# Two tiles of ternary weights move to the upper end of SBUF

## What is computed

```python
x = layernorm(x + attention0(x))      # causal softmax, 16 heads
x = layernorm(x + ffn0(x))            # ternary weights, below
x = layernorm(x + attention1(x))      # linear attention, relu features
x = layernorm(x + ffn1(x))            # plain weights

def ternarize(W):
    mask = abs(W) > 0.05 * max(abs(W))
    alpha = sum(abs(W) * mask) / max(sum(mask), 1)
    return alpha * sign(W) * mask     # alpha, 0 or -alpha

def ffn0(x):                          # W1 is 2048 x 512, W2 is 512 x 2048
    h = gelu(x @ ternarize(W1).T + b1)
    y = h @ ternarize(W2).T + b2
    scale = max(abs(y)) / 7 + 1e-8
    return clip(round(y / scale), -7, 7) * scale
```

## The kernel before

| phase | weights | activations | left over 512: weights, activations |
|---|---|---|---|
| qkv0 | p1_w_hi 33,472; p1_w_lo 58,048 | p1_xT_hi 90,816; p1_xT_lo 107,200 | 192, 192 |
| out0 | p3_w_hi 107,232; p3_w_lo 115,424 | p3_o_hi 140,000; p3_o_lo 156,384 | 224, 224 |
| ffn0 | tern 17,088 | p4_xT_hi 101,152; p4_xT_lo 117,536; p4_h_hi 138,016; p4_h_lo 142,112 | 192, 288 |
| linear attention | p5_w_hi 25,248; p5_w_lo 58,016 | p5_aT_hi 131,744; p5_aT_lo 148,128 | 160, 160 |
| ffn1 | p6_w0_hi 25,248; p6_w1_hi 90,784 | p6_xT 184,992; p6_h 203,424 | 160, 160 |

## Time and profile before

### The profile page before, as it was taken

One profiled execution on the slowest core, in us unless ns is written; L12 is line 12 of the kernel. 1 busy time (PEld: TensorE's weight loads), 2 busy tenths in 40 slices (PEclk: granted clock), 3 DMA queues, 4 the chain that ended last, 5 costly groups with the idle time before them and its releaser, 6 DMA issues. The chain is left out here.

```text
span 2647.1 us, 39886 instructions
## 1 busy us (share of the span) xinstructions
PE 2425.0 (92%) x12832; PEld 1797.7 (68%) x12832; DVE 1218.3 (46%) x2491; ACT 819.4 (31%) x1371; POOL 911.5 (34%) x1099
## 2 busy tenths in 40 slices
PE   7999699999999968599999994799999979999997
PEld 5888455555555436478888883588888858888886
DVE  3333477777777759611111112767677362111121
ACT  3222055555555531043344432111101112222221
POOL 0000156556556545233333332525153222222221
PEclk9999699999999988799999997899999989999999
DMA  6665735545544335400100103403212061000000
GB/s 246 226 226 191 175 91 126 120 117 122 126 117 117 80 109 190 147 17 32 48 32 32 32 16 111 148 33 126 95 63 95 9 202 49 32 32 32 32 33 32
DMA packets 154489, 255.29 MB, mean 96 GB/s; under 512 B 9648, under 2 KB 47536, under 8 KB 153904
## 3 DMA queue, kind: packets, MB, share of 16 engines
q1 hardware_dynamic: 137712, 208.20, 26.3%
q0 software_dynamic: 6144, 25.17, 2.9%
q10 hardware_dynamic: 10560, 20.97, 2.3%
HBM read 161.50 MB, written 92.27 MB: 96 GB/s over the span
## 5 line engine op out<-in xcount | busy, mean ns | idle before, releaser
L736 DVE CUSTOM_DVE_ANT_0 p_junk<-psum,p_causal 128x896 bf16<-128x896 f32 (+7 forms) x512 | 370.6, 752 | 159.2 <-PE psum L596 149.9
L699 ACT ACTIVATE p_probs<-psum 128x512 f32<-128x512 f32 (+1 forms) x640 | 331.3, 554 | 325.4 <-PE psum L607 319.9
L1130 POOL TENSOR_TENSOR p_h_lo<-p_h,p_h_hi 128x512 fp32r<-128x512 f32 x128 | 165.1, 1290 | 338.3 <-ACT p_h_hi L1159 338.3
L607 PE MATMUL psum<-p_qst,p_kst 98*128 98x512 f32 (+3 forms) x768 | 245.9, 384 | 17.3 <-ACT p_probs L699 10.9
L607 PEld LDWEIGHTS psum<-p_qst,p_kst 98*128 98x128 f32 x768 | 131.5, 190 | 170.3 <-ACT p_probs L699 84.8
L519 POOL TENSOR_SCALAR_AFFINE_SELECT p_probs<-p_probs 128x128 f32<-128x128 f32 x512 | 145.9, 305 | 263.8 <-ACT p_probs L699 263.0
L596 PE MATMUL psum<-p_kst,p_qst 96*128 96x512 f32 (+5 forms) x768 | 206.0, 369 | 20.5 <-DMA p_kst<-k_parts 17.0
L1762 POOL CAST p_h<-p_h 128x512 fp32r<-128x512 f16 x128 | 91.7, 716 | 372.9 <-ACT p_h L1786 372.9
L845 PE MATMUL psum<-p_xT_hi,tern 128*128 128x512 f32 x512 | 206.2, 403 | 1.4 <-DVE p_xT_lo L1224 1.4
L1195 PE MATMUL psum<-tern,p_h_hi 128*128 128x512 f32 x512 | 203.0, 397 | 2.2 <-POOL p_h_lo L1130 2.2
L845 PE MATMUL psum<-p_xT,p_w_hi 128*128 128x512 f32 x512 | 203.2, 397 | 0.7 <-ACT p_xT L1773 0.7
(11 more groups left out here) (174 smaller groups left out, 4764.2 us busy)
## 6 DMA issues: line engine op xcount, KB each, us to landing
p_qst<-q_parts SPq DMA_DIRECT2D x96, 256.0 KB, 4.6
p_kst<-k_parts SPq DMA_DIRECT2D x96, 256.0 KB, 6.9
q_parts<-p_qk_out SPq DMA_DIRECT2D x32, 512.0 KB, 2.8
k_parts<-p_qk_out SPq DMA_DIRECT2D x32, 512.0 KB, 2.8
ffn_x<-x SPq DMA_DIRECT2D x12, 1024.0 KB, 5.6
p_x<-in_x_t POOLq DMA_DIRECT2D x8, 1024.0 KB, 6.4
p_raw<-in_f_w POOLq DMA_DIRECT2D x8, 1024.0 KB, 7.9
v_rows<-p_v_out SPq DMA_DIRECT2D x32, 256.0 KB, 4.8
```

Of the source, the lines that this page charges most:

```text
L607: mm = pe.matmul(ST_BANKS[st % 2][:, col:col + CH - q0], kst[s][0:KD + 2, g, j * P:(j + 1) * P], qst[s][0:KD + 2, c, g, q0:CH], start=True ...
L699: act.activation(probs[:, n % 2, g, col:CH], ST_BANKS[st % 2][:, col:CH], ACT.Exp, scale=SM_SCALE).then_inc(p_ready, 1)
L736: dve.tensor_tensor_reduce(halves_of(junk[:, which, 0:n]), scores, halves_of(causal[:, SEQ - n:SEQ]), 1.0, FLOOR, ALU.add, ALU.max, rowmax ...
L1130: pool.tensor_tensor(h_lo[:, m % 2, :], h[:, m % 2, :], f32(h_hi[:, m % 2, :]), ALU.subtract).then_inc(hl_done, 1)
```

## The change

`tern` and `kept` are taken from the upper end of SBUF, downwards. All other tiles are taken from the lower end as before; those that came after `tern` and `kept` in the stack now start where `tern` started. No instruction, wait or size is changed.

```diff
             phase_qkv0(nc, psum, x_t, l0_wq, l0_wk, l0_wv, q_dram, k_dram, v_dram, ffn_w, w_max)
-            tern = sb("tern", [P, 2, KT * HID], F32R)
-            kept = sb("kept", [P, 2, 8, KT * HID // 64], F32)
+            far = lambda n, s, d: layer0.enter_context(nc.sbuf_tensor(n, s, d, side="right"))
+            tern = far("tern", [P, 2, KT * HID], F32R)
+            kept = far("kept", [P, 2, 8, KT * HID // 64], F32)
             alpha = sb("alpha", [P, 2], F32)
```

## The result

The changed kernel takes 2647.78 us, median of 22 runs (2645.57 to 2650.37), against 2651.32 us for the kernel before, also 22 runs (2649.72 to 2653.25). The ratio is 0.9986, 95% interval 0.998 to 0.9992. So it is faster, but by 3.5 us where 13.7 were forecast. That is inside what the forecast called "same", and inside its wide range, but not near its number. The profiled execution has a span of 2645.3 us, 1.8 less than before; its ffn0 begins 1.3 us later than before (first matmul at 1115.10 us against 1113.84), so not all of ffn0's gain shows in the span.

The account below looks back on a forecast made before the run. In ffn0 and ffn1 TensorE's start-to-start matmul time was taken as the bound. ffn0's 11.5 + 2.2 = 13.7 us off the profiled 2649.13 made 2635.4, plus 1.04 to the median 2636.5 us; 8-in-10 range 2633.5 to 2652.5.

Parts of the forecast that it names:

- same: Whole kernel: a time within about 0.2%, 5.3 us, of no change; chance 0.37.
- argument by exclusion: ffn0: 233.8 ns a matmul against ffn1's 226.6, laid to the operands' relative offset after other causes were ruled out.
- second sign: ffn1: first L845 group after transposes takes 1.93 us against 1.81, read as further support for the offset cause.
- rival of no change: ffn0: placement doesn't matter to TensorE, or 192 bytes are as bad as 96; 2650.2 us, chance 0.32.
- the last of the change's parts: ffn0: `tern` and partners come to lie 192 bytes apart, a multiple of 64, taken to gain the full pace.
- term of 13.7 us: ffn0: 100 plain steps gain 0.115 us each and 28 with transposes 0.08, 11.5 + 2.2 us.
- full gain: ffn0: all of the pace difference to ffn1 recovered, 13.7 us; chance 0.45.
- Half a cure: ffn0: offset 192 gives a pace between 226.6 and 233.8 ns, 7 us gained, 2643 us; chance 0.14.
- Worse than before: ffn0: 192 bytes apart collide more often than 96, up to 14.7 us more, 2665 us; chance 0.09.
- Zero for all else: Phases other than ffn0: cost 0; GpSimd's writes of `tern` 0.2 us if uncovered, VectorE's counts at most 0.1.

Follow-up runs that it names:

- e2: Kernel before, `tern` low as it was, 416 unused bytes ahead of p4_xT_hi so its ffn0 partners agree with it (offset 0); 2638.06 us against 2650.40.
- e3: Changed kernel with 288 unused bytes above `tern`, which stays high but has the offset of the kernel before; 2650.36 us against 2650.40.
- e1: Changed kernel with 192 unused bytes above `tern`, so it agrees with its ffn0 partners (offset 0); 2637.48 us against 2650.40 for the kernel before.
- e4: Kernel before with unused bytes around ffn1's xT and h, so they start 96 bytes off their plain weights; 2663.51 us against 2650.40.
- e6: Changed kernel with 128 unused bytes above `tern`, offset 64 to its partners; 2645.83 us against 2651.44, one run.
- e7: Changed kernel with 64 unused bytes above `tern`, offset 128 to its partners; 2648.59 us against 2651.44, one run.
- e8: Changed kernel with 448 unused bytes above `tern`, offset 256 to its partners; 2639.25 us against 2651.44, one run.
- e9: Changed kernel with 192 unused bytes above `tern` and 96 ahead of p4_h, so only ffn0's h tiles lie off `tern`; 2647.14 us against 2649.97.

## Why the prediction missed

- **What bounds ffn0, and that its pace is slow because of where the operands lie.** Right. The argument by exclusion (clock, other engines, DMA, loop, data, region) holds in each point that was tested: region by e2 and e3, data by e1 and e4, and the cause by e1, e2 and e4, which switch it off twice and on once, with 12.9, 12.3 and 13.1 us. Two of its supports were weaker than put. It counts out0 (224 and 224) among the fast phases, of which none of its rows speaks; the trace of the kernel before bears it out, with six matmuls in 1.37 us, 228 ns each:

```profile
1002.85 0.39 PE L845 MATMUL psum<-p_w_hi,p_o_hi 128*128 128x512 f32 x1
...
1004.22 0.39 PE L845 MATMUL psum<-p_w_hi,p_o_hi 128*128 128x512 f32 x1
```

  And the 1.93 us of the group after transposes were read as a second sign. Most of the excess over 1.81 lies in its first matmul, after which the next starts 0.32 us later; the other seven take 2257.53 - 2255.92 = 1.61 us, 230 ns each. That first matmul takes 0.31 to 0.32 us at each offset of ffn0, e1 and e2 included, so most of the excess has nothing to do with the offset. The kernel before:

```profile
2255.60 0.48 PE L845 MATMUL psum<-p_xT,p_w_hi 128*128 128x512 f32 x1
2255.92 0.39 PE L845 MATMUL psum<-p_xT,p_w_lo 128*128 128x512 f32 x1
```

- **The Trainium skill's rule** ("SBUF — State Buffer", "Who interferes with whom"), by which TensorE waits for no one, was named beside the rival of no change. The page speaks of engines that wait for each other and names no start bytes; the prediction took it to hold whatever the addresses. Read so, the runs contradict it: 192 bytes make 10 us between e1 and the changed kernel (2637.48 and 2647.78), 9.2 in the windows of ffn0. Whether TensorE waits for anything in there, no run shows.
- **The step that failed** is the last of the change's parts: "I take all of it, since 32 is the allocator's step and 64 the first multiple of it that tells the fast from the slow cases." The term of 13.7 us was sized by a period of 64 bytes. The table of starts said nothing for it: it held only offsets of 0 and 96 over 512, which periods of 128, 256 and 512 tell apart as well as 64 does. The period is 256 (e6, e7, e8), and 192 is not a multiple of it. The term measured 3.0 us of TensorE's time (497.11 to 494.14) in place of 13.7.
- **The size of the full gain** was nearly right: 13.7 forecast, 12.9 (e1) and 12.3 us (e2) measured, 12.2 and 13.2 in the windows of ffn0.
- **"Half a cure"** was the case that came: a pace between the two, 3.719 us a plain step in the mean. It was put at 7 us from a middle of two ends; the offset's own pace gives 0.021 us in each of some 100 plain steps, 2.1 us, and about 1 us in the 28 steps beside transposes (3.827 to 3.791 us in the mean), together the 3.0 of the windows. The case was named with a chance of 0.14, and its size had no row behind it.
- **Worse than before** did not come. No offset tried lies much above the kernel before: the highest is 497.52 us, at 96.
- **Zero for all else.** The windows show no other gain. GpSimd's write of `tern` went from 2375 to 2434 ns, 16 x 59 = 0.9 us where 0.2 was allowed, all of it beside TensorE in attention. In the traces of all ten experiments it takes 2379 to 2382 ns, eight of them with `tern` within 448 bytes of where the change puts it. So the region doesn't explain the 2434, which stand in one trace alone; the cause is open.

## What to carry to other kernels

Where two phases issue the same matmuls at the same granted clock, compare the time from start to start, not the busy share; TensorE was busy for 98% of ffn0 and 96% of ffn1, and the 7 ns a matmul show only in the starts. When fp32r matmuls of 512 columns set the pace, give their stationary and moving operands starts that agree over 256 bytes, that is, leave the same remainder when divided by 256; a small unused tile does it, and here e1 and e2 beat both kernels by it. Small tiles ahead of the operands (here `alpha` with 32 bytes and `b1` with 64, which make the 96) are enough to lose it for a whole phase. Other types and other numbers of columns were not tried at the full clock.

And when two facts fit several periods, write down each period with what it would make of the change, before one of them is taken: here 64 was taken where 128, 256 and 512 fitted too.

## What was not expected of the hardware

The pace of back-to-back fp32r matmuls depends on the distance between the starts of moving and stationary operand over 256 bytes: 3.63 us for 16 at distance 0, 3.72 to 3.74 at each other distance tried, all at a granted clock of 1.00. At the lower level, 1.2 GHz, no such difference shows in the one stretch of ffn0 that ran there, its first matmuls, where the granted clock is 0.50. The kernel before, at an offset of 160 over 256:

```profile
1121.80:1124.20 2.40, 2.40 (x7) 0.50 0.91 326
...
1122.23 0.63 PE L845 MATMUL psum<-p_xT_hi,tern 128*128 128x512 f32 x1
...
1123.08 0.63 PE L845 MATMUL psum<-p_xT_hi,tern 128*128 128x512 f32 x1
```

and e1, at offset 0:

```profile
1121.20:1123.40 2.20, 2.20 (x7) 0.50 0.79 308
...
1121.55 0.63 PE L845 MATMUL psum<-p_xT_hi,tern 128*128 128x512 f32 x1
...
1122.40 0.63 PE L845 MATMUL psum<-p_xT_hi,tern 128*128 128x512 f32 x1
```

Both take 0.85 us for two. And the pace has a memory: after matmuls that disagree, a group that agrees starts slower and is at the fast pace from its fifth matmul on (e9). After transposes, which stand behind the second half of a step and ahead of the next step, and not between the halves, a group that agrees takes 1.93 us, and the next one 1.82. Why the distance between the operands matters, no run here tells.
